# First step of gate and up in eight block products, and four places for the second norm's rows, in an attention and feed-forward kernel on one core

## What is computed

```
x = x + attn(layernorm(x))          # x is 8 x 1024 x 512
x = x + ffn(layernorm(x))
attn: kv = x @ W_to_kv.T; c = kv @ W_compress.T; ch = LN(c) * gamma + beta     (64 wide)
      q = ch @ W_q.T; k, v = split(ch @ W_kv.T); rope on q and k
      o = softmax(causal(q k.T / 8)) @ v
      z = o @ W_comp2lat.T;  out = z @ W_to_kv + z @ W_out_res.T + b_out_res
ffn:  h = silu(x @ W1.T) * (x @ W3.T)                   # W1, W3 are 2048 x 512
      out = fwht(h) @ W2.T                               # Walsh-Hadamard over 2048
```

## Time and profile before

| | us |
|---|---|
| median of 3 runs | 2113.64 |
| lowest, highest | 2111.71, 2113.83 |
| profiled execution, its own time | 2113.75 |
| profiled execution, span from first to last instruction | 2112.0 |
| TensorE busy | 2055.8 (97%) |
| VectorE busy | 1405.7 (67%) |
| ScalarE busy | 934.4 (44%) |
| GpSimd busy | 210.6 (10%) |

### The profile page before, as it was taken

How to read it: one execution, slowest core, us unless ns; L and a number is a source line. 1 busy time by engine, 2 the same in 40 slices (tenths; PEclk the granted TensorE clock), 3 DMA queues, 4 the chain that set the end, 5 groups by cost and what they waited for, 6 DMA issues and landing times. The chain is left out here.

```text
span 2112.0 us, 26777 instructions
## 1 busy us (share of the span) xinstructions
PE 2055.8 (97%) x9832; PEld 984.9 (47%) x9832; DVE 1405.7 (67%) x2674; ACT 934.4 (44%) x1431; POOL 210.6 (10%) x196
## 2 busy tenths in 40 slices
PE   6789999999999999999999999999999999999999
PEld 3434444444444444444444444444444444444444
DVE  7877888657676676766667676766767666653333
ACT  5857555344434444353543544435444444332221
POOL 2254641101001010011001010010100100000000
PEclk9899999999999999999999999999999999999999
DMA  8544246442463324633346323644146332363211
GB/s 333 208 182 155 103 145 159 156 139 77 119 165 125 128 83 132 158 120 119 110 130 168 116 94 110 153 154 136 60 134 174 124 121 87 112 158 110 90 59 71
DMA packets 231138, 278.62 MB, mean 132 GB/s; under 512 B 178016, under 2 KB 178144, under 8 KB 225632
## 3 DMA queue, kind: packets, MB, share of 16 engines
q1 hardware_dynamic: 231008, 276.91, 42.2%
HBM read 194.81 MB, written 39.85 MB: 111 GB/s over the span
## 5 line engine op out<-in xcount | busy, mean ns | idle before, releaser
L891 PE MATMUL PF<-XF,WS 128*128 128x512 f16 x1792 | 681.7, 380 | 10.9 <-DVE XF L1802 5.4
L892 PE MATMUL PF<-XF,WS 128*128 128x512 f16 x1792 | 680.2, 380 | 0.0
L893 PE MATMUL PF<-XF,WS 128*128 128x512 f16 x1792 | 680.1, 380 | 0.0
L915 PE MATMUL PD<-W2S,H 128*128 128x512 f16 x1024 | 388.6, 379 | 0.0
L916 PE MATMUL PD<-W2S,H 128*128 128x512 f16 x1024 | 388.6, 379 | 0.0
L917 PE MATMUL PD<-W2S,H 128*128 128x512 f16 x1024 | 388.4, 379 | 0.0
L1252 ACT ACTIVATE SH<-PF,afs 128x512 f32<-128x512 f32 x256 | 175.3, 687 | 373.7 <-PE PF L893 372.5
L1842 DVE TENSOR_TENSOR H<-SH,H 128x1024 f16<-128x1024 f32 x128 | 165.1, 1290 | 185.9 <-ACT H L1263 185.9
L891 PEld LDWEIGHTS PF<-XF,WS 128*128 128x128 f16 x1792 | 175.2, 98 | 237.2 <-issue 31.2
L893 PEld LDWEIGHTS PF<-XF,WS 128*128 128x128 f16 x1792 | 175.5, 98 | 212.0 <-issue 1.1
L1834 DVE SCALAR_TENSOR_TENSOR SH<-PF,afs,SH 128x512 f32<-128x512 f32 x256 | 191.7, 749 | 111.8 <-ACT SH L1252 97.9
(11 more groups left out here) (309 smaller groups left out, 1976.6 us busy)
## 6 DMA issues: line engine op xcount, KB each, us to landing
WS<-wscr SPq DMA_DIRECT2D x112, 896.0 KB, 4.9
W2S<-w2scr SPq DMA_DIRECT2D x30, 1024.0 KB, 6.5
ring<-x SPq DMA_DIRECT2D x56, 256.0 KB, 7.1
wscr<-WS SPq DMA_DIRECT2D x16, 896.0 KB, 3.8
out<-ring SPq DMA_DIRECT2D x56, 256.0 KB, 2.4
RAW<-w13t SPq DMA_DIRECT2D x16, 512.0 KB, 4.4
xraw<-xT SPq DMA_DIRECT2D x28, 256.0 KB, 5.8
XF<-w SPq DMA_DIRECT2D x13, 512.0 KB, 18.4
```

The costliest lines, as they stand in the source:

```text
L891: pe.matmul(bank, wh, th, start=i < 2 and j == 0, stop=False, skip_group_check=True)
L892: pe.matmul(bank, wh, tl, start=False, stop=False, skip_group_check=True)
L893: m = pe.matmul(bank, wl, th, start=False, stop=j == 1, skip_group_check=True)
L915: pe.matmul(PD[:, t % 2, :], th, wh, start=j == 0, stop=False)
```

## The change

Step k = 0 alone is computed in eight plain block products. Write the weights' blocks of a step as A11, A12, A21, A22 and the tokens' as blocks 0, 3, 7 and 5. Blocks 0 and 3 belong to tile 0, 7 and 5 to tile 1. Block 7 is new: it is tile 1's plain block, which so far was only used within differences; it shares its place in `XF` with block 6, which is therefore written later. `copy_b`, `copy_p5`, `sum_c` and `sum_e` fall away for step 0. A21 is not among the seven forms, since GpSimd overwrites it; it is now split by `a21_high` and `a21_low` into form 6's place of the tile `WS[:, 1]` before that, and `forms_high(1, 1)` waits until product group 4 has read it. Differences of tokens (blocks 1, 4, 2, 6) are wanted from step 1 on; their instructions move behind and into step 1. `norms` 13 go into the prologue, 14 and 15 partly into step 1; a check of ready rows (`norms_in`) replaces a wait for 26 norms. `SUMS_AT` goes from 10 to 12. The normed rows get four places `xs[t]`, and two of them are written earlier.

```diff
-XPLACE = ((0, 0), (0, 0), (0, 0), (0, 1), (1, 0), (1, 1), (0, 1))
+XPLACE = ((0, 0), (0, 0), (0, 0), (0, 1), (1, 0), (1, 1), (0, 1), (1, 0))
+XPART = (0, 1, 2, 3, 4, 5, 6, 6)
-SUMS_AT = 10
+SUMS_AT = 12
 def xf_no(s, i):
-    return 7 * s + ((0, 2, 4, 1, 3, 5, 6)[i] if s == 0 else i) + 1
+    return 7 * s + i + 2 if s else (0, 4, 6, 1, 5, 3, 7, 2)[i] + 1
+def wform_no(h, part):
+    return 2 * h + part + 2
-        xs = wsm[:, 0:512]
-        xs2 = half[:, 6144:7168].bitcast(F32)
+        xs = (wsm[:, 0:512], half[:, 6144:7168].bitcast(F32), SH[:, 0, :], hd)
# TensorE
+            def block_product(bank, f, i, first):
+                w.wait_ge(v_xf, xf_no(0, i))
+                for j in range(2):
+                    wh, wl = (WS[:, f == 2, m, (0, 1, 6, 3)[f], j * 128:(j + 1) * 128] for m in range(2))
+                    th, tl = (XF[:, m, XPART[i], :].rearrange("p (t f c) -> p f t c", t=4, f=2)[:, j] for m in range(2))
+                    pe.matmul(PF[:, bank, :], wh, th, start=first and j == 0, stop=False, skip_group_check=True)
+                    pe.matmul(PF[:, bank, :], wh, tl, start=False, stop=False, skip_group_check=True)
+                    m = pe.matmul(PF[:, bank, :], wl, th, start=False, stop=j == 1, skip_group_check=True)
+                return m
+            def first_step(j):
+                w.wait_ge(a_wh, wform_no(0, 1))
+                w.wait_ge(v_wl, wform_no(0, 1))
+                w.wait_ge(v_x2, 8)
+                if j < 4:
+                    m = block_product((1, 1, 0, 0)[j], j, (0, 3)[j % 2], j % 2 == 0)
+                elif j == 4:
+                    m = block_product(3, 2, 7, True)
+                elif j == 5:
+                    block_product(2, 0, 7, True)
+                    m = block_product(2, 1, 5, False)
+                else:
+                    m = block_product(3, 3, 5, False)
+                m.then_inc(p_gu, 1)
# ScalarE, in the prologue
+            def a21_high():
+                w.wait_ge(g_wm, 2)
+                w.wait_ge(a_sq, 4)
+                ac.activation(WS[:, 1, 0, 6, :], WF[:, 2, :], ACT.Copy).then_inc(a_wh, 1)
             hadamard(10)
+            square2(3)
+            a21_high()
             norms(6, 0)
             norms(6, 1)
-            square2(3)
             forms_high(0, 0)
...
             xtrans1(0, 2)
+            xtrans1(0, 3)
+            tokens_high(0, 0)
+            tokens_high(0, 3)
             norms(12, 0)
-            xtrans1(0, 3)
             norms(12, 1)
-            tokens_high(0, 0)
             xtrans1(1, 0)
+            norms(13, 0)
             xtrans1(1, 1)
-            tokens_high(0, 3)
+            norms(13, 1)
             xtrans1(1, 2)
             xtrans1(1, 3)
+            tokens_high(0, 7)
+            tokens_high(0, 5)
+            silu(0, 0)
+            tokens_high(0, 1)
# ScalarE, in the loop: k = 0: forms_high(1), tokens_high 4, silu(0,1), norms(14,0), tokens_high 2
#                       k = 1: copy_b, norms(14,1), high(0), norms(15,0), copy_p5, norms(15,1), tokens_high 6
# VectorE, in the prologue
+            def a21_low():
+                w.wait_ge(a_wh, 1)
+                ve.tensor_tensor(WS[:, 1, 1, 6, :], WF[:, 2, :], WS[:, 1, 0, 6, :], ALU.subtract).then_inc(v_wl, 1)
             parts_o1(1, 0)
+            a21_low()
             norm2(0)
...
             inverse1(1, 2)
+            xnorm1(0, 2)
             inverse1(1, 3)
             parts_o1(1, 1)
             factors(0, 4)
+            xnorm1(0, 3)
             outp1(1, 1)
...
-            xnorm1(0, 2)
             outp1(1, 3)
-            xnorm1(0, 3)
...
             tokens_low(0, 3)
+            tokens_low(0, 7)
+            tokens_low(0, 5)
             tokens_sum(0, 1)
             tokens_sum(0, 4)
             tokens_low(0, 1)
+            forms_low(1, 0)
+            forms_low(1, 1)
             tokens_sum(0, 2)
             tokens_low(0, 4)
-            tokens_low(0, 2)
-            tokens_low(0, 5)
# VectorE, in the loop: k = 1: hidden(0,0), tokens_low 2, tokens_sum 6, ..., sum_e(1), tokens_low 6, forms_low(2,1)
# GpSimd, forms(0)
+                if h == 0:
+                    w.wait_ge(a_wh, 1)
+                    w.wait_ge(v_wl, 1)
                 gp.tensor_tensor(WF[:, 2, :], WF[:, 0, :], WF[:, 2, :], ALU.subtract).then_inc(g_s, 1)
```

More of the change, by code:

```diff
@@ L345, in norm_row, with norms_in @@
             return rows[:, h % 7, :] if h < 13 else flat[:, o:o + 1024]
+        def norms_in(m, i):
+            slot = (7 * m + i) // 2
+            return 2 * (slot + 8 if slot < 6 else slot + 1)
         def xblock(s, i):
@@ L867, in product @@
                 bank = PF[:, (k % 2, 3, k % 2, 1 - k % 2, k % 2, 2, k % 2)[i], :]
-                if h == 0 and s == 0:
+                if k == 1:
                     w.wait_ge(v_xf, xf_no(s, i))
@@ L1023, in _ @@
                 for i in range(7):
-                    product(k, i)
+                    if k:
+                        product(k, i)
+                    else:
+                        first_step(i)
                     if i in (1, 3, 5, 6):
@@ L1417, in _ @@
                     fill(k - 1, 6)
-                copy_b(k)
+                if k:
+                    copy_b(k)
+                if k == 1:
+                    norms(14, 1)
                 if k:
                     high(k - 1)
-                if k == 0:
-                    for i in (1, 4, 2, 5):
-                        tokens_high(0, i)
+                if k == 1:
+                    norms(15, 0)
                 fill(k, 0)
-                copy_p5(k)
+                if k:
+                    copy_p5(k)
+                if k == 1:
+                    norms(15, 1)
+                    tokens_high(0, 6)
                 fill(k, 1)
@@ L1430, in _ @@
                 fill(k, 2)
-                silu(k, 0)
-                if k == 0:
-                    tokens_high(0, 6)
+                if k:
+                    silu(k, 0)
+                else:
+                    tokens_high(0, 4)
                 fill(k, 3)
@@ L1442, in _ @@
                     norms(14, 0)
-                    norms(14, 1)
+                    tokens_high(0, 2)
                 if k % 4 < 3:
                     fill(k, 6)
-                if k == 0:
-                    norms(15, 0)
-                    norms(15, 1)
             high(NK - 1)
@@ L2018, in _ @@
                         fill(k - 1, 6)
+                if k == 1:
+                    tokens_low(0, 2)
+                    tokens_sum(0, 6)
                 fill(k, 0)
@@ L2022, in _ @@
                 fill(k, 1)
-                sum_c(k)
                 if k:
+                    sum_c(k)
                     out_rows((k - 1) // 4 - 1, 2 * ((k - 1) % 4) + 1)
-                if k == 0:
-                    tokens_sum(0, 6)
                 fill(k, 2)
-                if s == 0 and h < NH - 1:
+                if k and s == 0 and h < NH - 1:
                     forms_low(h + 1, 0)
                 fill(k, 3)
-                sum_e(k)
-                if s == 0 and h < NH - 1:
+                if k:
+                    sum_e(k)
+                if k == 1:
+                    tokens_low(0, 6)
+                if k and s == 0 and h < NH - 1:
                     forms_low(h + 1, 1)
-                if k == 0:
-                    tokens_low(s, 6)
                 fill(k, 4)
```

86 lines of the change are left out of this document (49 added, 37 removed).

## The result

| | before | changed |
|---|---|---|
| median of 10 runs each on one chip, us | 2112.76 | 2118.2 |
| lowest, highest | 2111.16, 2113.97 | 2116.93, 2119.34 |
| span of the profiled execution | 2112.0 | 2116.0 |

Changed over before is 1.0025, 95% interval 1.0016 to 1.0033: 5.3 us slower (5.4 by the medians). 2114.1 had been forecast, with a range up to 2118 and 0.09 for "slower".

What follows compares the result with a forecast made beforehand. TensorE was taken as the bound far into the run, after early waits for VectorE, itself the bound until 160 us. +1.6, -5.9, +0.9 and +5.5 gave +2.1, absorbed to +0.5: 2114.1 us, range 2109 to 2118.

Steps and rivals of the forecast that it cites:

- +2.1 on PE: Sum of the terms up to `hadamard2(0)`: TensorE's lead of 3.4 us becomes a lag of 2.1, start at 130.0.
- Parts 1 and 2: Up to TensorE's first product: +2.65 and -1.0 us, so it starts 1.6 late, at about 96.5 instead of 94.95.
- Part 3: Step 0: eight products without a gap win 5.9 us; the second step's first product at 109.7, 4.3 ahead.
- Part 4: ScalarE in step 1: half norms and block 6's high half take back 0.9 us; latent transposes at 119.3, 3.4 ahead.
- Part 5: Before `hadamard2(0)`: `scale2` behind the next tile's statistics; TensorE waits 5.6 us, +5.5, then half rate behind it.
- The absorption: From `hadamard2(0)` to `scores(2,0)`: VectorE is level and bounds until 160 us, so TensorE's +2.1 us shrinks to +0.5.
- slower through the clock: Rival: the wait at 117 to 119 us also halves the clock; product (2,2) 5.4 late, end at 2119; chance 0.08.
- Part 1: Before the first product: VectorE waits 3.3 us for A21's high half, `a21_low` takes 0.42; +2.65 us.
- Part 2: Before the first product: four places let two row norms fill VectorE's waits, giving 1.0 us back.
- POOL holds DVE: Rival: GpSimd's earlier `forms(2)` beside VectorE's chain of blocks delays VectorE, some 2 us remain, end at 2116; chance 0.05.

Runs made afterwards that it cites:

- e6: Changed kernel with 22 idle matmuls (result unused) on TensorE ahead of `hadamard2(0)`: 2113.1 us, 1.0001 of the kernel before.
- e2: Changed kernel with `a21_low` moved on VectorE from before `norm2(0)` to behind `outp1(1,0)`: 2116.18 us, 1.0015 of the kernel before.
- e5: Changed kernel with A21's halves in free places of `WS[:, 1]`, high half made earlier, and `SUMS_AT` 10: 2110.1 us, 0.9985 of the kernel before.
- e8: Changed kernel with A21's halves in free places of `WS[:, 1]`, `SUMS_AT` left at 12: 2114.03 us, 1.0003 of the kernel before.
- e11: Changed kernel with A21's halves in free places, `SUMS_AT` 12, and 22 idle matmuls ahead of `hadamard2(0)`: 2109.61 us, 0.9981 of the kernel before.
- e7: Kernel before with only the four places for rows and the two moved row norms: 2113.95 us, 1.0006 of the kernel before.
- e10: Changed kernel with 22 idle matmuls ahead of `hadamard2(0)` and 10 more ahead of the latent transposes: 2113.06 us, 1.0000 of the kernel before.
- e1: Changed kernel with `SUMS_AT` back at 10, nothing else: 2113.29 us, 1.0006 of the kernel before.
- e4: Kernel before with `SUMS_AT` 12 and nothing else of the change: 2115.42 us, 1.0011 of the kernel before.
- e12: Changed kernel with 44 already met waits on TensorE, between `hadamard2(0)`'s two waits, no idle matmuls: 2114.56 us, 1.0013 of the kernel before.
- e13: Changed kernel with A21's halves in free places, `SUMS_AT` 10, and 44 already met waits at TensorE's start: 2108.15 us, 0.9978 of the kernel before.
- e3: Changed kernel with `SUMS_AT` 10 and `a21_low` moved behind `outp1(1,0)`: 2111.6 us, 0.9993 of the kernel before.

## Why the prediction was wrong, step by step

**The step that failed is the sum up to `hadamard2(0)`, "+2.1 on PE".** It came to +6.3, and its terms are what was mis-sized (us, from the table above):

| | forecast | measured |
|---|---|---|
| Parts 1 and 2, first product | +1.6 | +3.5 |
| Part 3, eight products | -5.9 | -6.6 |
| Part 4, to the latent transposes | +0.9 | +2.3 |
| Part 5, to `hadamard2(0)` | +5.5 | +7.1 |
| sum | +2.1 | +6.3 |
| taken up until `scores(2,0)` | -1.6 | -1.8 |
| left | +0.5 | +4.5 |

Counted from the cast, the first term is +4.5 and 5.5 us are left, near the 5.3 of the ratio.

The absorption itself held. Product (2,2) was to be 2.9 late and was 7.0 late; until `scores(2,0)` 2.5 of it was taken up, where 2.4 had been forecast. TensorE's waits for `split2` shrank as was said, from 3.0 to 0.2:
```profile
PE PD L861 <- DVE afs L1855: 5.6, 1, 5.6
...
PE XY L676 <- ACT PB L1109: 2.9, 1, 2.9
...
PE PD L861 <- DVE W2S L1863: 0.2, 1, 0.2
```
The shift was to lie between VectorE's own and TensorE's, nearer VectorE's, and it did. But VectorE was to be level (`split2(0)` at 132.7), and `split2(0)` ran at 137.00. The timelines of VectorE and ScalarE after say why:
```profile
137.00 0.75 DVE L1863 SCALAR_TENSOR_TENSOR W2S<-PD,afs,W2S 128x512 f16<-128x512 f32 x1 [2.34 <-ACT W2S L1242]
```
```profile
136.28 0.69 ACT L1242 ACTIVATE W2S<-PD,afs 128x512 f16<-128x512 f32 x1 [8.89 <-PE PD L861]
```
VectorE waited for ScalarE, and ScalarE for `hadamard2(0)`. That was 4.2 later than forecast, and `split2(0)` 4.3.

The rival "slower through the clock" was to decide from product (2,2) at 139.1; it came at 141.97, and the end at 2118.2 was near the rival's 2119. It had 0.08 because a wait of 1.77 had left the clock up; the wait here was 2.87, and the clock fell behind it. Still, the rival had only part of the cause: it charged 2.5 to this half rate, and 1.5 was measured (Part 5). The other 2.6 of the 4.2 came with the late transposes. That its end was so near is in part luck. The half rate behind `hadamard2(0)`, which the forecast had counted, is worth 1.5 us (e6).

**Part 1, A21 (+2.65).** The wait and the operation were right (3.3 and 0.42):
```profile
65.79 0.43 DVE L1870 TENSOR_TENSOR WS<-WX,WS 128x256 f16<-128x256 f32 x1 [3.56 <-ACT WS L1255]
66.13 0.37 DVE L1700 BATCH_NORM_AGGREGATE st<-st 128x2 f32<-128x6 f32 x4
66.54 0.59 DVE L1704 TENSOR_SCALAR st<-st 128x4 f32<-128x4 f32 x1
67.17 0.65 DVE L1540 TENSOR_SCALAR st<-st 128x4 int32<-128x4 int32 x1
...
68.05 0.55 DVE L1530 TENSOR_TENSOR st<-st 128x4 f32<-128x4 f32 x1
```
Mis-sized was what follows: three operations of the norm, 0.14 to 0.17 each before, took 0.55 to 0.65 beside GpSimd's adds, which start when `a21_low` ends, 1.3 us in all. In e2, where the adds run later, they take 0.14 to 0.17 again. Counted from the cast, `forms_low(0,0)` starts 4.0 late and not 2.65. Measured: 3.2 to 4.2 by the medians, up to 4.6 by the ratios (e5, e6, e8, e11). In e5 the three operations are as slow (0.56 to 0.66), but `forms_low(0,0)` is only 0.5 late from the cast: without the wait for the square they fall for the most part into the 1.07 us that VectorE had idled there.

**Part 2, the places (-1.0).** Worth nothing in the kernel before (e7); not tried alone in the changed one. With Part 1 the first product was to be 1.6 late and was 3.5.

**Part 3, the eight products (-5.9).** Right: 6.6.

**Part 4, ScalarE (+0.9).** Mis-sized: the lead shrank from 3.1 to 0.8, by 2.3. ScalarE began copy_b at 113.20 (forecast 111.1): TensorE's second step was 1.2 later than forecast, and VectorE, for which it then waited, was held up:
```profile
109.49 2.29 DVE L1881 TENSOR_TENSOR XF<-XS,XF 128x1024 f16<-128x1024 f32 x1
...
114.16 1.75 DVE L1891 TENSOR_TENSOR XS<-XS 128x1024 f32<-128x1024 f32 x1
115.83 1.74 DVE L1924 TENSOR_TENSOR H<-SH,H 128x1024 f16<-128x1024 f32 x1
```
```profile
108.61 4.31 POOL L2165 TENSOR_TENSOR WX<-RAW,sc 128x512 f32<-128x512 f32 x2 [4.15 <-DVE WS L1875]
112.99 1.83 POOL L2167 TENSOR_TENSOR WX<-WX 128x256 f32<-128x256 f32 x1
```
Later ScalarE stood 0.72 us more for the last of GpSimd's adds. Timeline of ScalarE:
```profile
119.00 1.79 ACT L1266 ACTIVATE WS<-WX 128x1024 f16<-128x1024 f32 x2 [0.72 <-POOL WX L2176]
```
A low half takes 1.22 alone and 2.29 beside GpSimd, whose two products take 4.31 (3.33 in the earlier trace rows) and an add 1.83 (0.72). "POOL holds DVE" was a rival with 0.05, set aside on seven rows of which one touched GpSimd's work, and there GpSimd gave way. The Trainium skill (SBUF — State Buffer, Who interferes with whom) has it that a VectorE operation with two inputs in SBUF contends with GpSimd's reads; these rows agree. Its price alone wasn't measured.

**Part 5, up to `hadamard2(0)` (+5.5).** From 0.8 ahead to 6.3 late, 7.1. The wait was as forecast (5.6). `scale2` ended at 134.1 and not at 129.95, since `sum_e(1)` ahead of it ran at 125.22, not at 121.1, after a wait of 1.69 for TensorE's late product (1,4):
```profile
125.22 0.70 DVE L1903 TENSOR_TENSOR PF<-PF,p 128x512 f32<-128x512 f32 x1 [1.69 <-PE PF L911]
```
Of these 4.1 us, 2.6 are the latent transposes (121.89, not 119.3), which Parts 1 to 4 account for. The other 1.5 are the term that Part 5 put at nothing: behind the wait of 2.87 the transposes and product (1,4) ran at half rate (122.44 to 124.97, 2.5 us in the place of 1.3). e10, with the clock kept there, has `hadamard2(0)` 10.9 us behind the transposes, e6 12.1. The late scale as a whole costs 4.9, 3.9 and 2.7 (changed less e1, e8 less e5, e4 less before), by the ratios 4.0, 3.8 and 2.3.

**Open.** e12 puts e6's gain of 5.1 as 3.6 from the code's place and 1.5 from the clock; by the ratios it is 2.5 and 2.6, and the intervals allow both. The profiles speak for the first: up to `scores(2,0)` e6 gains 1.5 from its first product on and e12 nothing, and behind it they gain 3.0 and 3.3. The kernel before has such a late transfer too (near 452 us), so the code's place is no part of the 5.3 between the kernels: it only stood in the way of reading e6. What GpSimd's overlap costs at the end was argued from rows only. And the clock of step 0 is not the same in each execution of the old first step: in the earlier trace rows TensorE was at the full rate from 103.60 on, but in the profile of e4, whose step 0 has the same instructions, at half rate until 108.2, and in that of e7 likewise:
```profile
102.73 0.61 PE L891 MATMUL PF<-XF,WS 128*128 128x512 f16 x1 [0.72 <-DVE XF L1802]
```
There the latent transposes come 29.8 us behind the first product, in the earlier trace rows's execution 27.7. So the steps measured against that one execution (Parts 3 and 4 above all) can be 2 us off for another; the medians over many runs hold both kinds.

The fastest version is e13 (0.9978, 4.6 us under the kernel before): eight products, `SUMS_AT` 10, A21 in free places, code moved. e11 (0.9981), with the late scale and the clock kept, can't be told from it.

## What to carry to other kernels

When a change moves an operation back on its engine, add up every lateness on the way to it: a wait, operations slowed by a neighbour and a product at half rate were each small, and all of them arrived at the one wait behind it, 4.2 us over the forecast. A lowered clock that is counted behind one long wait is worth a term behind the other long waits too. An operation that two engines must read before a third overwrites it belongs where none of them has to wait for its place. And an experiment that adds instructions moves code: run the same count of empty instructions beside it before a gain is put down to what they do.

## What the hardware showed that was not expected

A 16 KB packet of TensorE's code within a transposing transfer made it land after 4.1 us in the place of 2.5, and TensorE's wait of 0.7 became 2.3 with half rate behind it. Moving the code by 44 instructions took 2.0 and 3.6 us off two kernels (1.5 and 2.5 by the ratios, where only the second is at the edge of the noise); the wait fell from 2.2 or 2.3 to 0.7 in both. Small VectorE operations (128x4) beside GpSimd took 0.55 to 0.65 in the place of 0.14 to 0.17. TensorE's clock was full behind a wait of 2.88 us ahead of the latent transposes in e3 and of 2.44 in e5 (0.46 for the four, 0.38 a matmul behind them), and half behind one of 2.07 there in e11 (0.60 and 0.61 to 0.63): how long the last wait was does not tell it alone. Behind a wait of 0.72 us in step 0 the clock was full in the kernel before (0.39) and half in e4 (0.61), at the same instruction.
